# State-space rows of a macaron block: a fourth place for padded x, and the order of one copy, one norm and one pair's sums

## What is computed

```python
x = x + 0.5 * ffn(layernorm(x))
x = x + mamba(layernorm(x))
x = x + 0.5 * ffn(layernorm(x))
```

```python
x, z = split(transpose(hidden @ W_in))
x = gelu(dwconv_same(x, K_x, b_x))          # 4 taps, needs x padded on both sides
z = gelu(dwconv_same(z, K_z, b_z))
dt, B, C = split(x.T @ W_xproj)
delta = softplus(dt @ W_dt + b_dt)
h[t] = exp(delta[t] * A) * h[t-1] + delta[t] * B[t] * x[t]     # 16 states for each of 128 channels
y[t] = sum over states (h[t] * C[t]) + x[t] * D
out = concat(y, z).T @ W_out
```

## Time and profile before

| | us |
|---|---|
| median of 3 runs (857.1 to 858.07) | 857.6 |
| the profiled execution, whole | 857.62 |
| its span | 855.9 |
| TensorE busy in the span | 827.8 (97%) |
| VectorE busy | 682.5 (80%) |
| GpSimd busy | 649.9 (76%) |
| ScalarE busy | 556.1 (65%) |
| mean granted clock of TensorE | 0.997 |

### The profile page before, as it was taken

One profiled execution on the slowest core, in us unless ns is written; L12 is line 12 of the kernel. 1 busy time (PEld: TensorE's weight loads), 2 busy tenths in 40 slices (PEclk: granted clock), 3 DMA queues, 4 the chain that ended last, 5 costly groups with the idle time before them and its releaser, 6 DMA issues. The chain is left out here.

```text
span 855.9 us, 12885 instructions
## 1 busy us (share of the span) xinstructions
PE 827.8 (97%) x3952; PEld 642.8 (75%) x3952; DVE 682.5 (80%) x1280; ACT 556.1 (65%) x1019; POOL 649.9 (76%) x474
## 2 busy tenths in 40 slices
PE   8999999999999999999999987999999999999997
PEld 7678787887887686576666766887887888788885
DVE  6969767776976678999999999997876977776664
ACT  6575565565565757899998894466565556555553
POOL 6958775776674767999999999676776677576765
PEclk9999999999999999999999999999999999999999
DMA  8644474446434341856465664527175446536440
GB/s 218 211 130 119 131 189 112 151 117 169 123 103 124 98 127 62 292 210 210 165 232 198 229 213 155 174 69 208 61 219 165 124 134 166 152 108 175 134 124 25
DMA packets 127573, 131.08 MB, mean 153 GB/s; under 512 B 59528, under 2 KB 83216, under 8 KB 127504
## 3 DMA queue, kind: packets, MB, share of 16 engines
q1 hardware_dynamic: 104800, 125.00, 47.5%
q10 hardware_dynamic: 22704, 5.25, 2.9%
HBM read 120.78 MB, written 9.44 MB: 152 GB/s over the span
## 5 line engine op out<-in xcount | busy, mean ns | idle before, releaser
L817 POOL TENSOR_TENSOR act_lo<-act,act_hi 128x512 fp32r<-128x512 f32 x288 | 372.6, 1299 | 185.6 <-ACT act_hi L928 183.5
L921 ACT ACTIVATE bank<-bank 128x512 f32<-128x512 f32 x252 | 146.7, 582 | 231.3 <-PE bank L1255 219.9
L1151 DVE TENSOR_TENSOR sg<-bank,c_ring 128x512 f32<-128x512 f32 x252 | 172.7, 685 | 95.5 <-ACT bank L921 92.9
L1251 PE MATMUL bank<-x_parts,w_hi 128*128 128x512 f32 x572 | 230.4, 403 | 3.2 <-DVE sg L1151 1.9
L1129 DVE SCALAR_TENSOR_TENSOR act<-sg,bank 128x512 f32<-128x512 f32 x288 | 197.7, 687 | 40.3 <-PE bank L1255 19.9
L1255 PE MATMUL bank<-x_parts,w_hi 128*128 128x512 f32 x572 | 226.2, 395 | 0.0
L1252 PE MATMUL bank<-x_parts,w_lo 128*128 128x512 f32 x572 | 226.1, 395 | 0.0
L928 ACT ACTIVATE act_hi<-act 128x512 fp32r<-128x512 f32 x286 | 178.1, 623 | 0.8 <-PE bank L1227 0.4
L1251 PEld LDWEIGHTS bank<-x_parts,w_hi 128*128 128x128 f32 x572 | 107.5, 188 | 34.3 <-issue 3.8
L1255 PEld LDWEIGHTS bank<-x_parts,w_hi 128*128 128x128 f32 x572 | 107.5, 188 | 26.0
L1252 PEld LDWEIGHTS bank<-x_parts,w_lo 128*128 128x128 f32 x572 | 107.6, 188 | 24.8 <-issue 0.7
(11 more groups left out here) (183 smaller groups left out, 1020.0 us busy)
## 6 DMA issues: line engine op xcount, KB each, us to landing
c_ring<-c_dram SPq DMA_DIRECT2D x252, 256.0 KB, 3.7
c_ring<-c_dram SPq DMA_DIRECT2D x64, 512.0 KB, 4.4
b_slots<-c_dram SPq DMA_DIRECT2D x16, 512.0 KB, 5.0
y_dram<-out_t SPq DMA_DIRECT2D x56, 64.0 KB, 2.8
y_tok<-y_dram SPq DMA_DIRECT2D x14, 256.0 KB, 3.8
xt_dram<-xn ACTq DMA_DIRECT2D x40, 64.0 KB, 3.5
xt<-xt_dram ACTq DMA_DIRECT2D x10, 256.0 KB, 3.6
out<-x_sb SPq DMA_DIRECT2D x7, 256.0 KB, 2.5
```

What stands on the lines that cost most here:

```text
L817: self.nc.gpsimd.tensor_tensor(m["act_lo"][:, g % LAG], m["act"][:, g % ACTS], m["act_hi"][:, g % LAG].bitcast(FP32), ALU.subtract).then_i ...
L921: nc.scalar.activation(self.h_bank[:, g % 2], self.h_bank[:, g % 2], ACT.Silu).then_inc(self.sg_ready, 1)
L1151: nc.vector.tensor_tensor(m["sg"][:, g % 2], silu, weight, ALU.mult).then_inc(self.w_done, 1)
L1251: nc.tensor.matmul(dst, m["w_hi"][:, k, n, :], x_hi, start=True, stop=False)
```

## The change

`x_pad` gets a fourth place, so the copy of row r waits for the z convolution of row r - 4 and no longer for that of row r - 3. On ScalarE the copy of row i + 3 stands ahead of the second decays of step n = 7 (pair 1 of the next row). The norm of row 3 stands in step n = 4 of row 0 in place of n = 5, between the decays of its two moved pairs. On TensorE, in step n = 6, the transposes of row i + 3 and the z convolution's last two taps stand ahead of the sums of pair g - 3. The row in `x_pad` that later takes z of the last row becomes 5 % 4.

```diff
+X_SLOTS = 4
-        x_pad = sb("x_pad", [P, 3, SEQ + TAPS - 1])
+        x_pad = sb("x_pad", [P, X_SLOTS, SEQ + TAPS - 1])
 def act_copy_xt(self, ae, r, src):
     ae.wait_ge(self.norm.xt_ready, BATCH + r + 1)
-    need(ae, self.conv_z, r - 2)
-    self.nc.scalar.activation(self.m["x_pad"][:, r % 3, 1:SEQ + 1], src, ACT.Copy).then_inc(self.xt_copied, 1)
+    need(ae, self.conv_z, r - X_SLOTS + 1)
+    self.nc.scalar.activation(self.m["x_pad"][:, r % X_SLOTS, 1:SEQ + 1], src, ACT.Copy).then_inc(self.xt_copied, 1)
...
 def act_pairs(self, ae, front):
...
+                if n == 7 and i + 3 < BATCH:
+                    self.act_copy_xt(ae, i + 3, self.misc)
                 if RING <= g + 1 < ALL_PAIRS and self.moved(g + 1):
                     self.act_decays(ae, g + 1)
                 if RING <= g + 2 < ALL_PAIRS and not self.moved(g + 2):
                     self.act_decays(ae, g + 2)
...
-                if n == 5 and i == 0:
+                if n == 4 and i == 0:
                     self.norm.act_apply(ae, BATCH + 3)
...
-                if n == 7 and i + 3 < BATCH:
-                    self.act_copy_xt(ae, i + 3, self.misc)
                 if n == 7 and i + 2 < BATCH:
                     self.act_gelu_u(ae, i + 2, self.front[:, 0, :])
...
 def pe_pairs(self, pe):
...
+                if n == 6 and i + 3 < BATCH:
+                    need(pe, self.x_added, i)
+                    self.norm.pe_transpose(pe, BATCH + i + 3, self.misc)
+                if n == 6 and i < BATCH - 2:
+                    self.pe_conv(pe, i, 1, [2, 3], self.z_bank(i))
                 if SUM_LAG <= g <= ALL_PAIRS - PAIRS + 1 and (n or i == BATCH - 1):
                     self.pe_add_states(pe, g - SUM_LAG)
...
-                if n == 6 and i + 3 < BATCH:
-                    need(pe, self.x_added, i)
-                    self.norm.pe_transpose(pe, BATCH + i + 3, self.misc)
...
-                    if n == 6:
-                        self.pe_conv(pe, i, 1, [2, 3], self.z_bank(i))
```

More of the change, by code:

```diff
@@ L1568, in z_row @@
             return self.z
-        return self.m["u"][:, (BATCH - 3) % 3] if i == BATCH - 2 else self.m["x_pad"][:, (BATCH - 3) % 3, 0:SEQ]
+        return self.m["u"][:, (BATCH - 3) % 3] if i == BATCH - 2 else self.m["x_pad"][:, (BATCH - 3) % X_SLOTS, 0:SEQ]
     def z_bank(self, i):
@@ L1823, in pe_conv @@
         for k in taps:
-            last = nc.tensor.matmul(dst, m["w_tap"][:, h, k, :], m["x_pad"][:, r % 3, k:k + SEQ],
+            last = nc.tensor.matmul(dst, m["w_tap"][:, h, k, :], m["x_pad"][:, r % X_SLOTS, k:k + SEQ],
                                     start=(k == 0), stop=(k == TAPS - 1), skip_group_check=True)
```

## The result

The changed kernel takes 859.03 us (median of 18 runs, 858.1 to 859.97) against 857.27 us (18 runs, 856.72 to 858.07): the ratio is 1.0020, with a 95% interval of 1.0014 to 1.0027. That is 1.76 us slower, in the range given (856.6 to 860.3), at the edge of what was called no change, and on the side that was forecast; the forecast of +1.0 us was 0.8 us too small.

A forecast was written before the change was run, and what follows sets the result against it. VectorE's chain of scans was taken to bound the state-space rows. Lost 1.24 + 2.76 = 4.00 us, won 1.88 + 1.10 = 2.98, net +1.0 on 857.62: 858.6 us, range 856.6 to 860.3.

The forecast's parts named there:

- What bounds the stage: State-space rows: VectorE's chain of scans sets the end; a microsecond won or lost there moves the second expert part's start.
- The idle that goes: VectorE's waits before pairs 9 and 10 (1.88 us), 26 (0.54) and 42 (0.56) vanish: 2.98 us won.
- Row 0: Pair 7's scan waits for the sums of pair 3, put behind transposes and two taps: 1.24 us lost.
- Rows 1 to 4: Scans of pairs 15, 23, 31 and 39 wait for TensorE's later sums: 0.69 us per row, 2.76 us lost.
- The sum: Lost 4.00 us, won 2.98 us: net +1.0 us on 857.62, so 858.6, a small loss counting as no change.
- the lower bound: If the taps cost only 1.32 us: row wait 0.30, row 0's 0.85, net -1.0, so 856.6 us.
- Row 5: TensorE has taps but no transposes and no `x_added` wait there; sums at T + 15.9, just in time.
- the copy in rows 1 to 3: ScalarE's copy and second decays change places within an unbroken run: nothing gained; the later decays covered by some 5 us.
- the spread and sums of step n = 7: TensorE's work behind step n = 6 comes 0.4 us later, into a pause before the B, C product; nothing more late.
- That the sums are in time: Rival, chance 0.12: the sums end before VectorE needs them, nothing of the 4.00 us is lost; 855.7 us.
- That ScalarE's gain does not reach VectorE: Rival, chance 0.06: pair 10's decays stay put because delta of row 2 waits for TensorE; +1.6 us, 859.2.
- The longer waits: Rival, chance 0.14: waits for sums of 1.1 us per row, 1.6 in row 0, 0.3 in row 5; +3.3, 860.9.

The follow-up runs named there:

- the version with the sums first: The changed kernel with TensorE's step n = 6 back in its old order: sums of pair g - 3, then transposes, then taps; 856.94 us against 857.2, ratio 0.9995.

## Why the prediction was right, and where it was off

- *What bounds the stage.* Right for a loss: with +1.61 us at the last scan the runs are 1.76 slower, with +2.98 (TensorE's order alone) 3.4. Not right for a gain: "a microsecond won or lost on VectorE moves the start of the second expert part" failed at a gain of 1.46 us, of which 0.84 were lost again at pair 62. I had left out that TensorE has stretches at half its clock there, and had called GpSimd a follower.
- *The idle that goes.* I had 1.88 + 0.54 + 0.56 us; the ledger has 1.95, 0.54 and 0.57. The decays of pair 10 start at 366.26 in the changed kernel, as forecast before VectorE can use them. The 1.88 us stood under the norm, however, and the norm alone moved pair 10 by 0.49; the size was right because all parts of the change were there.
- *Row 0.* Forecast 1.24 us, measured 1.34.
- *Rows 1 to 4.* The step that was mis-sized is the 0.69 us per row; it measured 0.86 to 0.89, 3.49 us for four rows in place of 2.76. Term by term in row 2: the transposes started 13.58 us after pair 17's scan, where I had 13.55; they took 0.49 to the taps, not 0.43, the first of them having to load its weights after the release; taps 1.72 for 1.71; sums 1.04 for 1.03; and the release from TensorE's sums to VectorE took 0.13, not the 0.05 taken over from other pairs of engines. Together 0.19. That TensorE waits for the copy, that the cover of the sums is gone, and that the sums then release the scan, all came out.
- *The sum.* Row 0 lost 0.10 more, rows 1 to 4 0.73 more; 0.08 more were won back, and 0.11 at pair 62. The ledger gives +1.6 where I had +1.0; the runs give +1.76. The runs ended at the edge of what I had called no change (859.03, where "slower" began at 859.3); with terms 0.8 us too small in sum, that this word was right is in part luck. Two sums are off without effect: a row on VectorE is 25.37 us, not 25.36, and the lower bound counts the waits before pairs 26 and 42 as wholly won (2.05 - 2.98 = -0.93) in the same sentence that keeps them in part, so that the edge of 856.6 was too low.
- *Row 5, the copy in rows 1 to 3, the spread and sums of step n = 7*: no wait of VectorE there, as forecast.
- *The rivals.* That the sums are in time is what the version with the sums between transposes and taps brings about, and it gives 856.9, not the 855.7 that I had worked out; in its trace pair 10 came 0.44 us sooner and not 1.88, behind the late transfer to GpSimd, and what held back the other runs is open. That ScalarE's gain does not reach VectorE did not happen. The longer waits did come, at 0.86 to 0.89 us a row, a little short of the 0.9 from which I had let that rival decide.

The page "TensorE: Matmul & The Clock Gate" of the Trainium skill (Back-to-back issue gap), by whose spacing the two taps would last an estimated 0.5 us, does not describe these fp32 matmuls: the changed kernel shows 1.72 us again, and one tap taken from ahead of the sums took 0.87 us off the wait before pair 7.

## What to carry to other kernels

Before putting work ahead of an instruction on a busy in-order engine, look for who waits for that instruction and how much room it has (here 1.89 us between the sums and the scan), and count what the moved work will now wait for itself, since the cover it had has moved behind it. Waits in one loop do not add up: a wait earlier in the row had already paid part of the later one, so undoing the largest single wait (1.34 us) gave 0.9. And when a gain disappears on the way to the end, look at the granted clock in short windows before naming the engine that took it: here a mean of 0.997 over the whole span hid a stretch at half speed, which cost 0.84 us in one version, 0.11 in the kernel before and nothing in others, by where it lay. A version that removes work can move that stretch too, and then it tests two things at once.

## What was not expected of the hardware

In nine of the twelve traces TensorE's granted clock is at 0.50 for some microseconds, at another place in each but always between 519 and 537 us, and at 1.00 in all the rest of the state-space rows; in the other three it stays at 1.00 throughout. TensorE's sums of one pair (eight matmuls) take 1.91 us there, against 1.03 to 1.04. TensorE had just waited 2.60 us when the clock fell in the version with the sums first, and 1.54 to 1.90 us a little earlier in the kernel before and in the changed one; but a wait of 2.58 us in the version with the sums between transposes and taps was not followed by a fall. What brings it about is not shown.

The release of a VectorE scan by TensorE's sums took 0.13 us in rows 0 to 4 of the changed kernel (359.02 to 359.15 in row 0, 411.51 to 411.64 in row 2; the ends of TensorE's work are modelled by the profiler), whereas ScalarE's copy released TensorE in 0.05 us (408.21 to 408.26). Transposes that start right at a release took 0.49 us up to the next matmuls, against 0.43 to 0.44 when TensorE comes to them busy; their weight loads start at the release as well (408.26), so in this trace nothing was loaded ahead of the wait.
